# First attention of a fused attention and expert kernel: division moved behind the value product, softmax sums from matmuls, value product in 32-column tiles

## Reference

```python
x = x + _L0_xattn_ref(_layernorm(x, axis=-1), ctx_768, Wq, bq, Wkv, bkv, Wo, bo)
# in it, with 16 heads of 16 features and m = 77 keys
q = (einsum('bld,ed->ble', x, Wq) + bq).reshape(b, l, h, dh)
kv = (einsum('bmc,ec->bme', y, Wkv) + bkv).reshape(b, m, h, 2 * dh)
att = softmax(einsum('blhd,bmhd->blmh', q, k) * scale, axis=2)
out = einsum('blmh,bmhd->blhd', att, v).reshape(b, l, d)
return einsum('bld,ed->ble', out, Wo) + bo
```

## Time and profile before

| | |
|---|---|
| median of 3 runs | 885.13 us (884.46 to 886.65) |
| the profiled execution | 889.84 us |
| its span, first to last instruction | 887.7 us |
| mean granted TensorE clock | 0.895 of full |
| stage A's 32 units | from 24.57 to 171.17 us of the span |

### The profile page before, as it was taken

One profiled execution on the slowest core, in us unless ns is written; L12 is line 12 of the kernel. 1 busy time (PEld: TensorE's weight loads), 2 busy tenths in 40 slices (PEclk: granted clock), 3 DMA queues, 4 the chain that ended last, 5 costly groups with the idle time before them and its releaser, 6 DMA issues.

```text
span 887.7 us, 10616 instructions
## 1 busy us (share of the span) xinstructions
PE 724.3 (82%) x3332; PEld 417.2 (47%) x3332; DVE 584.6 (66%) x1732; ACT 294.8 (33%) x641; POOL 355.8 (40%) x372
## 2 busy tenths in 40 slices
PE   4689877864798998989979866868798899999972
PEld 3456544562344444444547623323253374647651
DVE  3888887435756373462657788999795497664265
ACT  2354333210372451815412253555420212021210
POOL 2344434103588685685410246787700021112020
PEclk9999999955898997988979977998889799999996
DMA  8910000210122221121288100020010000000002
GB/s 219 400 31 1 1 12 3 80 62 24 53 72 72 69 81 49 65 81 58 78 256 317 44 2 0 1 95 1 0 48 0 1 1 0 1 0 1 0 1 95
DMA packets 33086, 52.77 MB, mean 59 GB/s; under 512 B 8718, under 2 KB 21582, under 8 KB 32776
## 3 DMA queue, kind: packets, MB, share of 16 engines
q1 hardware_dynamic: 28040, 36.76, 12.6%
q0 software_dynamic: 4992, 15.34, 5.1%
HBM read 36.62 MB, written 15.47 MB: 59 GB/s over the span
## 4 chain that ended last, share of the span: by engine, by line
PE 54%; DVE 25%; POOL 6%; issue 6%; ACT 5%; DMA 2%; POOLq 1%; SPq 0%; DVEq 0%; ACTq 0%
PE ps L459 50%; DVE arena L1883 4%; DVE arena L1880 3%; ACT arena L934 2%; DVE arena L1496 2%; DVE arena L1492 2%; DVE arena L329 2%; DMA arena<-scr_z,idsU 2%; DVE kp L1385 1%; DVE arena L1385 1%; DVE arena L1391 1%; POOL arena L1274 1%; POOL scr_g L1266 1%; PE ps L514 1%; DVE X L1391 1%
## 5 line engine op out<-in xcount | busy, mean ns | idle before, releaser
L459 PE MATMUL ps<-arena 64*32 64x32 f32 (+6 forms) x2296 | 543.6, 396 | 29.9 <-DVE arena L1609 8.7
L459 PEld LDWEIGHTS ps<-arena 128*128 128x128 f32 (+3 forms) x2296 | 267.3, 164 | 231.5 <-issue 182.7
L934 ACT ACTIVATE arena<-ps 128x256 f32<-128x256 f32 (+6 forms) x255 | 120.5, 487 | 280.5 <-PE ps L459 136.0
L324 POOL TENSOR_SCALAR rstd<-mv 128x4 f32<-128x4 f32 (+2 forms) x34 | 14.6, 430 | 236.8 <-DVE mv L318 183.4
L1736 DVE TENSOR_TENSOR arena<-ps,arena 128x512 f32<-128x512 f32 x39 | 27.0, 691 | 103.3 <-ACT arena L1048 91.1
L1232 POOL TENSOR_TENSOR arena<-arena 128x616 f32<-128x616 f32 x32 | 40.2, 1256 | 80.0 <-DVE arena L1504 80.0
L1266 POOL DMA_INDIRECT scr_g<-arena,destU x39 | 50.1, 1285 | 37.7 <-DVE arena L1736 30.4
L1259 POOL DMA_INDIRECT arena<-scr_z,idsU x39 | 45.9, 1177 | 40.8 <-PE ps L652 28.7
L1883 DVE MATCH_REPLACE8 arena<-arena 128x77 f32<-128x77 f32 x256 | 54.1, 222 | 0.0
L1048 ACT ACTIVATE arena<-ps 128x512 f32<-128x512 f32 x39 | 23.3, 597 | 92.2 <-PE ps L459 92.0
L988 ACT ACTIVATE arena<-arena 128x616 f32<-128x616 f32 x32 | 23.0, 717 | 75.7 <-DVE arena L1496 75.7
(11 more groups left out here) (196 smaller groups left out, 988.9 us busy)
## 6 DMA issues: line engine op xcount, KB each, us to landing
arena<-in_w1t SPq DMA_DIRECT2D x8, 1024.0 KB, 14.0
arena<-scr_g SPq DMA_DIRECT2D x8, 1024.0 KB, 7.9
X<-in_x SPq DMA_DIRECT2D x2, 1024.0 KB, 5.9
scr_z<-arena SPq DMA_DIRECT2D x4, 512.0 KB, 3.3
arena<-in_c_dftf SPq DMA_DIRECT2D x1, 2048.0 KB, 14.9
arena<-in_L_xattn_W SPq DMA_DIRECT2D x2, 1024.0 KB, 6.3
out<-X SPq DMA_DIRECT2D x16, 128.0 KB, 1.8
scr_k<-arena SPq DMA_DIRECT2D x4, 256.0 KB, 8.2
```

Source lines behind the costliest of these rows:

```text
L459: return pe.matmul(o, l, r, start=first, stop=final)
L934: return a.activation(o, i, ACT.Copy)
```

## The change

The probabilities are no longer divided before the transposes. GpSimd's product, VectorE's sum and its small reciprocal go, 32 of each. In their place a second set of matmuls, `sums`, multiplies `PT` with a matrix `sk` of zeros and ones (the head mask, spread by one VectorE copy into `mblk`, transposed by five transposes `turn_s` and copied by `put_s`), so that PSUM bank 7 holds each head's sum on the rows of its features. VectorE takes the reciprocal of the whole 128 x 512 bank and multiplies bank 6 with it into `OT` (`divide`); ScalarE's `put_o` goes. `values` and `sums` are each eight matmuls of 512 columns with a stationary operand of 32 columns, for two heads at a time: two rounds r over the four 32-row strips q of the bank, since the 154 keys of two heads lie in two chunks. The lag goes from three to two, `Pb` has three buffers in place of four, the scores stay as they were, and the second half of the queries moves from st = 6 of the block before to st = 0 of its own. The orders of all engines are written anew.

```diff
             def turn_P(u):
-                pe.wait_ge(s["probs_norm"], u + 1)
+                pe.wait_ge(s["probs_exp"], u + 1)
...
-            def values(j, g, chunks):
-                for c in chunks:
-                    if c == 0:
-                        pe.wait_ge(s["pt_sb"], turned_all(8 * j + 4 * g + 3))
-                        pe.wait_ge(s["vk_sb"], 5)
-                        pe.wait_ge(s["oT_sb"], 2 * j + g)
-                    m = vkeys(c)
-                    ins = mm(bank(6), vk[0:m, j // 2, g, c, :], PT[0:m, g, c, :], c == 0, c == NCH - 1)
+            def values(j, g):
+                pe.wait_ge(s["pt_sb"], turned_all(8 * j + 4 * g + 3))
+                for r in range(2):
+                    for q in range(4):
+                        m, cols = vkeys(q + r), slice(32 * q, 32 * q + 32)
+                        ins = mm(ps[cols, 6, :], vk[0:m, j // 2, g, q + r, cols], PT[0:m, g, q + r, :], r == 0, r == 1)
+                ins.then_inc(s["oT_ps"], 1)
+
+            def sums(g):
+                for r in range(2):
+                    for q in range(4):
+                        m, cols = vkeys(q + r), slice(32 * q, 32 * q + 32)
+                        ins = mm(ps[cols, 7, :], sk[0:m, q + r, cols], PT[0:m, g, q + r, :], r == 0, r == 1)
+                ins.then_inc(s["oT_ps"], 1)
...
-            queries(0, 1, 6)
-            pe.wait_ge(s["qT_sb"], 2)
-            for S in range(NU + 3):
+            for S in range(NU + 2):
...
+                if st == 0:
+                    if j:
+                        pe.wait_ge(s["oT_sb"], 2 * j - 1)
+                    queries(j, 1, 7)
...
                 elif st == 2:
+                    if j:
+                        values(j - 1, 1)
                 elif st == 3:
+                        sums(1)
+                elif st == 4:
+                        project(j - 1, 0)
                 elif st == 5:
+                        project(j - 1, 1)
                 elif st == 6:
+                    values(j, 0)
                 elif st == 7:
+                    sums(0)
...
-            for u in range(NU):
-                p.wait_ge(s["probs_sum"], u + 1)
-                p.tensor_tensor(pv, pv, smA[:, u % 4, :].unsqueeze(2).broadcast_to([P, HG, S2]), ALU.mult)\
...
+            def divide(j, g):
+                v.wait_ge(s["oT_ps"], 2 * (2 * j + g) + 2)
+                if j:
+                    v.wait_ge(s["oA_ps"], 2 * j)
+                own.done(v.reciprocal(OT[:, g, :], bank(7)))
+                own.settle()
+                v.tensor_tensor(OT[:, g, :], bank(6), OT[:, g, :], ALU.mult).then_inc(s["oT_sb"], 1)
...
+                if j and st == 3:
+                    divide(j - 1, 1)
...
+                elif st == 7:
+                    divide(j, 0)
```

More of the change, by code:

```diff
@@ L50 @@
 ARENA = 37144
+PBUF = 3
 SCAT = 4
@@ L562, in _ @@
                     scores_A(S)
-                if S >= 3:
-                    turn_P(S - 3)
+                if S >= 2:
+                    turn_P(S - 2)
                 if 1 <= S <= 5:
                     turn_v(S - 1)
[L567 to L573, removed]
-                elif st == 2:
-                    if j:
[L576 to L580, removed]
-                elif st == 3:
-                    if ahead:
-                        pe.wait_ge(s["zTA_sb"], 2 * j + 3)
-                        turn_z(j + 1, 1, 7)
-                    if j:
[L586 to L590, removed]
@@ L591, in _ @@
                 elif st == 6:
                     if j:
[L593 to L596, removed]
+                        pe.wait_ge(s["xA_done"], 2 * j - 1)
+                    else:
+                        pe.wait_ge(s["vk_sb"], 7)
+                    values(j, 0)
                 elif st == 7:
                     if j:
-                        if ahead:
-                            pe.wait_ge(s["qT_sb"], 2 * j + 4)
-                        project(j - 1, 0)
@@ L602, in _ @@
-                    values(j, 0, (0,))
-            values(NBLK - 1, 1, range(NCH))
-            pe.wait_ge(s["xA_done"], 2 * NBLK - 2)
+                        pe.wait_ge(s["xA_done"], 2 * j)
+                    sums(0)
+            turn_P(NU - 1)
+            pe.wait_ge(s["oT_sb"], 2 * NBLK - 1)
+            values(NBLK - 1, 1)
+            sums(1)
             project(NBLK - 1, 0)
@@ L994, in _ @@
[L994 to L1007, removed]
+                    if st == 0:
+                        put_q(j, 1, 7)
@@ new lines, in _ @@
+                    if st == 1 and ahead:
+                        put_z(j + 1, 0, 7)
+                        if j:
+                            put_z(j + 1, 1, 6)
+                    if st == 2 and ahead:
+                        if j:
+                            put_q(j + 1, 0, 7)
+                        else:
+                            put_z(1, 1, 7)
+                    if S == 3:
+                        put_q(1, 0, 7)
+                    if S in (4, 5):
+                        put_s(S - 4)
@@ L1227, in _ @@
             rstd_A(1)
-            for u in range(NU):
-                j, st = u // 8, u % 8
-                p.wait_ge(s["probs_sum"], u + 1)
-                pv = Pb[:, u % 4, :].rearrange("p (h k) -> p h k", h=HG)
-                p.tensor_tensor(pv, pv, smA[:, u % 4, :].unsqueeze(2).broadcast_to([P, HG, S2]), ALU.mult)\
[L1233 to L1241, removed]
+            p.wait_ge(s["rows_in"], 16 * 9)
+            for j in range(NBLK):
+                if j >= 2:
+                    rstd_A(j)
+                for t in range(4):
+                    bias_A(4 * j + t)
+            if "B" in stages:
+                rstd_B(0)
+                rstd_B(1)
             if "B" in stages:
@@ L1452, in add_A @@
                 v.wait_ge(s["xbA"], n + 2)
-                v.tensor_tensor(X[:, n:n + 2, :], X[:, n:n + 2, :], bank(7).rearrange("p (t n) -> p t n", t=2), ALU.add)\
+                v.tensor_tensor(X[:, n:n + 2, :], X[:, n:n + 2, :], bank(6 + pair).rearrange("p (t n) -> p t n", t=2), ALU.add)\
                     .then_inc(s["xA_done"], 1)
```

149 lines of the change are left out of this document (88 added, 61 removed).

## The result

| | before | changed |
|---|---|---|
| median | 884.8 us (882.15 to 888.65, 14 runs) | 895.47 us (887.21 to 899.44, 14 runs) |
| ratio | | 1.0103, 95% interval 1.0079 to 1.0126 |
| span of the profiled execution | 887.7 us | 897.4 us |
| unit 0's first scores to the last `add_A` | 24.6 to 171.1: 146.5 us | 22.1 to 184.2: 162.1 us |
| of stage A at half of the full clock | 3.4 us | 30.7 us |

The kernel became slower by 1.0%; the forecast was 883 us, 0.2% faster. The profiled execution of the changed kernel took 899.44 us, the longest of its fourteen runs and 4 us above their median; what follows is read from it, so it shows rather more of the loss than a typical run has. The page answers to the earlier trace rows: GpSimd lost 41 us of work, VectorE next to nothing, and its eight large reciprocals take 3358 ns each.

A forecast was written before the change was run, and what follows sets the result against it. TensorE was taken as the bound of stage A, VectorE close behind. Start -3.6, block 1 +4.2, block 2 -0.8, block 3 and end -3.1, and 1.1 for slower `project` gave -2.2 us: median 885.13 becomes 883, range 868 to 912.

The forecast's parts named there:

- The 2.8 us gaps: TensorE standing for `divide` twice a block, ahead of `queries(j, 1)` or `project`; 2.8 us each, taken as harmless to the clock.
- last doubt: Last condition listed for the forecast being wrong: the 2.8 us gaps cost the clock; no size given.
- the 1.1 for the last one: End of stage A: the last `divide` makes a TensorE gap, so `project` matmuls run slower; 1.1 us added.
- the range of 868 to 912: Range for the whole kernel's time in us, leaving out rival 3 and the far side of rival 4.
- the chance of 0.47 for slower: Chance that the changed kernel measures slower, beside 0.37 for faster and 0.16 for the same.
- X: Time TensorE takes for one set of eight narrow matmuls of `values` or `sums`; 1.75 us, four strips working together.
- the change of form: TensorE going in and out of the narrow form; 0.1 us a set.
- Rivals 1 to 4: On X: 1 half price only, 3.45 (0.25); 2 strips staggered, 2.2 (0.10); 3 no gain, 6.9 (0.08); 4 both, 0.9 (0.15).
- A block: Blocks 1 and 2 of stage A after the change: 29.1 us without waits, 34.5 with the waits for `divide`.
- Block 3 with the end: Last part of stage A, from block 3 to the last addition: 48.4 us, against 51.5 before.
- the start: Unit 0 to unit 8: scores 2.2 us earlier, VectorE 1.9 less; 3.6 taken, unit 8 at 50.5 instead of 54.1.
- The sum: Stage A: start -3.6, block 1 +4.2, block 2 -0.8, block 3 and end -3.1, together -3.3; net -2.2 us.

The follow-up runs named there:

- experiment 1: The changed kernel with idle float32 matmuls of 128 columns ahead of each TensorE wait for `divide`; 882.67 us, 0.9939 of the kernel before.
- experiment 5: The changed kernel with one unit's scores and transposes moved ahead of each wait for `divide` at st = 0 and 4; 878.01 us, 0.9931 of the kernel before.
- experiment 3: The changed kernel with the reciprocal of the bank of sums replaced by a copy, which leaves out the division; 863.15 us, 0.9744 of the kernel before.
- 4: The kernel before with only `values` as narrow sets, the division staying on GpSimd and the lag three; 880.09 us, 0.9919 of the kernel before.
- 6: The changed kernel with scores and transposes moved ahead, and second-half queries waiting only until the reciprocal has read its bank; 878.89 us, 0.9928 of the kernel before.
- experiment 2: The changed kernel with `values` and `sums` as five full-width matmuls each in place of the narrow sets; 928.83 us, 1.0475 of the kernel before.
- experiment 7: The changed kernel with five idle matmuls ahead of each wait for `divide` in the blocks, nine at the end; 885.0 us, 0.9985 of the kernel before.

## Why the prediction was wrong

**The step that failed** is "The 2.8 us gaps I take as harmless, as `turn_P` waited up to 2.6 in stretches whose clock stayed at 1.00". Two gaps in stretches that happened to keep their clock were taken for a bound. They were 2.33 and 2.6 us and neither was followed by half clock; the changed kernel's 2.42 us were, five times in six. The prediction did name this as its last doubt ("or if the 2.8 us gaps cost the clock") and gave it no price and no chance. The price stood in the earlier trace rows: 3.4 us at half clock, up to 1.7 lost for each gap. Eight gaps at 1.7 would have been 13.6 in place of the 1.1 for the last one, and the forecast 895.5. That this is the measured median to the tenth is luck: measured are seven of eight, 11.7 us (changed kernel against experiment 1), and 2.6 more in the start, with other errors and the scatter of the later stages on top. Luck too is that 895.5 lies in the range of 868 to 912: the range, and the chance of 0.47 for slower, came almost wholly from rivals on X, and X was right.

The Trainium skill ("TensorE: Matmul & The Clock Gate", "HAM oscillation — how this bites in real kernels") describes this as a mode of its own: bursts of matmuls with waits between them send the clock down and up again at each wait, and its cure is to reorder the loop so that more matmuls stand together ahead of a wait. The rule that the section gives would let waits as short as these pass; here 2.42 us were enough five times in six, and the measurement decides. Otherwise the trace agrees with the mode, since eight of the nine stretches in stage A come with a wait of 1.99 us or more, and experiment 5 agrees with the cure.

**Right, and measured as forecast:**
- X, on which all was said to hang: 1.75 and 0.1 for the change of form, measured 1.86 to the next weight load and 1.96 with what the next scores lose. The four strips work together in float32; in the records of a set the four start 6 to 7 ns apart (up to 12 where the last has 104 rows). Rivals 1 to 4 all fell.
- The reciprocal of a whole bank, worked out as linear in the columns from 203 and 953 ns: 3.35, measured 3.358. The product: 0.69, as in the earlier trace rows.
- The place of the waits: two a block, ahead of `queries(j, 1)` and of the first `project`; 2.8 forecast, 2.42 measured. The waits of the earlier trace rows went.
- A block: 34.5 forecast, 34.7 and 34.8 in experiment 1; without waits 29.1, and 29.4 in experiment 3. Block 3 with the end: 48.4, and 48.5 in experiment 1.

**Wrong in size, beside the clock:** the start. Scores of unit 0 began 2.4 us earlier (22.15 against 24.57), for 2.2 forecast. But from there to unit 8 the forecast had 1.4 us less than before, 28.1, and it takes 29.8 in experiment 1 at full clock. The 29.5 of the kernel before even hold a stretch at half clock, up to 1.7 us. What the forecast's start left out stands in the kernel: `values(0, 0)` and `sums(0)` now run ahead of unit 8, two sets at 1.96, where the kernel before had one piece at 0.86, and the transposes `turn_s` came in. TensorE is busy without a gap just there in experiment 1, from 45.0 to 52.3 us:

```profile
45.00:52.30 7.30, 7.30 (x51) 3.43 (x51) 3.84 (x6) 3.23 (x6) 2.13 (x3) 1.00 0.37 68
```

No run tells how much of the miss this is. In the changed kernel the start took 32.4, with two stretches at half clock, the second behind a gap of 2.15 us that the kernel before doesn't have.

**The sum again**, for the end of stage A: forecast 171.2 - 2.2 = 169.0. Measured 184.2, 15.2 later. The clock is 12.8 of it: 184.2 less the 170.3 of experiment 1, less the 1.1 allowed for. The start is 1.8 (52.3 for 50.5) and the blocks and the end 0.6. Over the whole kernel the ratio stands for 9.1 us and the medians lie 10.7 apart, against 13.1 at the end of stage A. In the profiled executions 3.4 us of that come back in the stages behind, within their scatter. Four of the fourteen runs of the changed kernel took 887 to 889 us, the others 895 to 899, 8.6 us more in the mean. They have no trace, but their mean granted clock is on record: 0.893 to 0.897 for the four, 0.879 to 0.887 for the others. The means lie 0.0117 apart, which over 895 us is 21 us less at half clock, worth up to 10.4 us and so enough for the 8.6. So the same instructions can lose most of this or not; in which stage the four gained isn't shown.

**The direction.** The moved division gained nothing for VectorE, as forecast (583.3 against 584.6 us in the whole kernel): it turned 32 small sums and 32 small reciprocals, spread over the units, into eight lumps of 4.1 us that TensorE waits for. What the narrow tiles earned was lost in these, first as waits (5.3 us a block: 34.7 less 29.4) and then again as clock (3.4 a block: 38.1 less 34.7).

## What to carry to other kernels

Where a change puts a wait of a few microseconds on the matmul engine, price it as the wait and half the slow stretch that can follow, with a chance; that a gap of this length is once seen at full clock is no bound. Then look for work of the next unit that can stand ahead of the wait, as it fills the gap and keeps the clock, where filler matmuls only keep the clock. Gathering many small operations that run beside another engine's work into a few large ones saves no time when that engine must wait for the last one to end. A division that is moved behind a product is dear or cheap by its shape: here the reciprocal was paid by the column.

## What the runs showed of the hardware

- A gap's length alone did not tell whether TensorE's clock falls. The plainest case is the start: the same instructions stand ahead of the same gap of 2.15 us in the changed kernel and in seven experiments (all but 4), and 3.4 us at half clock followed in three of the eight (changed, 5, 6). In the changed kernel five of six gaps of 2.42 us were followed, in experiment 2 four of six of 2.59. A gap of 1.99 was followed in the changed kernel and not in experiments 5 and 6. One of 2.58 near 33 us was followed in experiment 7 and not in experiment 3. In stage A the longest, 2.89 to 4.27 us, were always followed; never followed were those of 2.33 and 2.6 in blocks 1 to 3 of the kernel before, six of 1.31 in experiment 7 and those of 0.84 and 1.28 in experiment 5. One stretch of the changed kernel, at 35.6 us, had no longer gaps just ahead than 1.53 and 0.88.
- Matmuls of 128 columns whose result nobody reads held the clock at 1.00 and took nothing from VectorE or ScalarE: their busy times in block 1 are 25.65 and 13.63 without them, 25.66 and 13.59 with them.
- Eight float32 matmuls of 512 columns in four 32-column strips take 1.86 us, or 1.96 with what the next matmuls lose, against 1.72 for two at full width by the earlier trace rows.
- The reciprocal on VectorE takes 203 ns for 8 columns, 953 for 128 and 3358 for 512, the last read from PSUM: 6.25 ns a column throughout. The product of the 512-column shape takes 691 and a copy 692 ns.
